# Product 1 of a two-product kernel written out in another order, with its row and column sums taken elsewhere

## The reference, cut to what matters

```python
# x (2, 1024, 2048), ctx (2, 2048, 2048), all float32; s1, z1, s2, z2, g1, g2 are scalars
def fake_quant(x, s, z):
    return (clip(round(x / s + z), 0, 255) - z) * s
x = x + tanh(g1) * matmul(fake_quant(layernorm(x), s1, z1), fake_quant(ctx, s2, z2))   # product 1
h = layernorm(x)
base = h @ base_W.T                                          # (2048, 2048): product 2
logits = h @ router_W.T                                      # 8 experts, the best two are kept
mid = einsum('bsd,edr->bser', h, lora_A) * weights_of_the_best_two
inc = einsum('bser,erd->bsd', mid, lora_B)
out = x + tanh(g2) * (base + 2.0 * inc)
```

## Time and profile before

| | |
|---|---|
| median of 3 runs | 1163.9 us (1162.96 to 1165.37) |
| span of the profiled execution | 1164.5 us (the profile gives no other time of its own for it) |
| PE busy in the span | 1085.9 us, 93% |
| DVE, ACT, POOL busy | 594.8 us, 297.2 us, 189.4 us |
| first unit of product 1 starts | 34.67 us |
| last unit of product 1 ends, product 2's first transposes start | 306.2 us |
| PE busy in the 271.6 us between | 237.9 us |

### The profile page before, as it was taken

The page is one execution under the profiler, slowest core; times in us unless marked ns, Lnnn a source line. Parts: engine busy times, 40 slices in busy tenths (PEclk is TensorE's granted clock), DMA queues, the critical chain, the costliest instruction groups (busy, mean ns, idle before and its releaser), DMA issues.

```text
span 1164.5 us, 13520 instructions
## 1 busy us (share of the span) xinstructions
PE 1085.9 (93%) x5130; PEld 816.5 (70%) x5152; DVE 594.8 (51%) x876; ACT 297.2 (26%) x291; POOL 189.4 (16%) x123
## 2 busy tenths in 40 slices
PE   1678987989999999998999999989999999999998
PEld 1333433334688888887888887878888789888887
DVE  7999698976763543343237224334533343222231
ACT  6642344310241212231112113111211321111210
POOL 3766678662300000000000000000000000000000
PEclk9999998999999999999999999999999999999999
DMA  9885997647572633507242633351542614162440
GB/s 361 299 298 179 311 327 224 236 147 256 190 262 67 200 116 105 194 23 291 73 153 70 211 99 118 132 212 55 181 144 73 199 40 142 54 203 84 148 145 37
DMA packets 111051, 193.88 MB, mean 166 GB/s; under 512 B 30608, under 2 KB 32656, under 8 KB 106896
## 3 DMA queue, kind: packets, MB, share of 16 engines
q1 hardware_dynamic: 68368, 153.18, 38.1%
q10 hardware_dynamic: 42624, 39.85, 11.0%
HBM read 153.16 MB, written 33.55 MB: 160 GB/s over the span
## 4 chain that ended last, share of the span: by engine, by line
PE 71%; DVE 10%; issue 6%; POOL 6%; DMA 4%; ACT 1%; SPq 1%; ACTq 0%; DVEq 0%; POOLq 0%
PE acc L818 17%; PE acc L820 17%; PE acc L819 17%; PE acc L795 3%; POOL ctx_quant L380 3%; PE acc_even L818 3%; PE acc_even L819 3%; PE acc_even L820 3%; DMA w_stage<-in_wt 2%; DVE bn_chunks L540 2%; DVE ctx_tree_sums L591 2%; PE aT_psum L855 1%; PE aT_psum L856 1%; POOL x_group_odd L394 1%; PE aT_psum L833 1%
## 5 line engine op out<-in xcount | busy, mean ns | idle before, releaser
L818 PE MATMUL acc<-w_hi,hT_hi 128*128 128x512 f32 x896 | 353.8, 395 | 0.0
L820 PE MATMUL acc<-w_hi,hT_lo 128*128 128x512 f32 x896 | 350.3, 391 | 0.0
L819 PE MATMUL acc<-w_lo,hT_hi 128*128 128x512 f32 x896 | 349.9, 390 | 0.0
L667 DVE TENSOR_TENSOR w_lo<-w_stage,w_hi 128x1024 fp32r<-128x1024 f32 x128 | 156.6, 1224 | 320.7 <-ACT w_hi L476 318.6
L476 ACT ACTIVATE w_hi<-w_stage 128x1024 fp32r<-128x1024 f32 x128 | 135.6, 1059 | 460.3 <-PE acc L820 314.2
L820 PEld LDWEIGHTS acc<-w_hi,hT_lo 128*128 128x128 f32 x896 | 168.8, 188 | 35.9
L819 PEld LDWEIGHTS acc<-w_lo,hT_hi 128*128 128x128 f32 x896 | 169.0, 189 | 34.2
L818 PEld LDWEIGHTS acc<-w_hi,hT_hi 128*128 128x128 f32 x896 | 168.8, 188 | 33.9
L795 PE MATMUL acc<-ctx_quant,aT_even 128*128 128x512 bf16 x501 | 121.2, 401 | 10.4 <-DVE x_group_even L611 7.9
L795 PE MATMUL acc<-ctx_quant,aT_odd 128*128 128x512 bf16 x501 | 113.7, 383 | 5.0 <-DVE x_group_odd L611 4.4
L795 PEld LDWEIGHTS acc<-ctx_quant,aT_even 128*128 128x128 bf16 x512 | 52.0, 103 | 77.5 <-issue 21.8
(11 more groups left out here) (129 smaller groups left out, 1011.8 us busy)
## 6 DMA issues: line engine op xcount, KB each, us to landing
w_stage<-in_wt SPq DMA_DIRECT2D x128, 512.0 KB, 5.8
ctx_stage<-in_ctx SPq DMA_DIRECT2D x32, 1024.0 KB, 6.5
x_group_even<-x_scratch SPq DMA_DIRECT2D x16, 1024.0 KB, 10.4
residual<-x_scratch SPq DMA_DIRECT2D x64, 256.0 KB, 4.0
out<-residual ACTq DMA_DIRECT2D x64, 256.0 KB, 2.8
x_group_even<-in_x SPq DMA_DIRECT2D x8, 1024.0 KB, 9.0
x_group_odd<-in_x SPq DMA_DIRECT2D x8, 1024.0 KB, 8.1
x_scratch<-x_group_even ACTq DMA_DIRECT2D x8, 1024.0 KB, 4.9
```

What stands on the lines that cost most here:

```text
L667: dve.tensor_tensor(wl[s][:, :], wst[s][:, :], wh[s][:, :].bitcast(F32), ALU.subtract)\
L818: pe.matmul(out_, lh, rh, start=first, stop=False)
L819: pe.matmul(out_, lh, rl, start=False, stop=False)
L820: return pe.matmul(out_, ll, rh, start=False, stop=final)
```

## The change

The change replaces the tables and touches these parts:

- The units come in another order. Before, all four tiles of a group meet block 0, then block 1, and so on. Now the order mixes tiles and blocks within a batch (`UNIT_TILE`, `UNIT_BLOCK`), and the banks go round by position. The loads of SP are in an order of their own (`LOAD_ORDER`).
- Rows: the widening of 8 of the 16 tiles (3, 4, 5, 6, 11, 13, 14, 15) is an ACTIVATE with a row sum on ACT instead of a TENSOR_SCALAR on DVE. The small instruction for the row term stays on DVE and is now apart (`row_sum`). `a_rows` and `x_u8` have two buffers each.
- Three tiles instead of four are transposed on PE; the other 13 by DMA.
- Columns: DVE makes only the first of the four tree instructions (4096 wide, `pair`), and eight matmuls with ones, added up in PSUM, replace the one. The column term is kept for each of the four blocks of a batch, so it is made 8 times instead of 16.

```diff
-PE_TILES = 4
+PE_TILES = 3
+WIDEN_ACT = [3, 4, 5, 6, 11, 13, 14, 15]
+LOAD_ORDER = 'xcxccxccccxccxcccxccccxxccccxcxcxcxcccxccxcxcccx'
+UNIT_TILE = [0, 1, 2, 1, 2, 0, 3, 2, 3, 0, 4, 1, 0, 5, 3, 3, 1, 2, 5, 6, 7, 5, 4, 7, 6, 6, 7, 6, 7, 4, 5, 4, 8,
...
+UNIT_BLOCK = [0, 0, 0, 1, 1, 1, 1, 2, 0, 2, 2, 2, 3, 1, 2, 3, 3, 3, 0, 1, 3, 3, 0, 0, 0, 2, 1, 3, 2, 3, 2, 1, 4,
...
-        anat = at("a_rows", SMALL, [P, D], BF16)
-        xu8 = at("x_u8", SMALL + 4 * KIB, [P, D], U8)
-        csum = at("ctx_part_sums", SMALL + 6 * KIB, [P, NB, NW], F16)
-        tree = at("ctx_tree_sums", SMALL + 10 * KIB, [P, K // 2, NW], F16)
-        colb = [at(f"col_term{s}", SMALL + 18 * KIB + 2 * KIB * s, [P, NW], F32) for s in range(2)]
+        anat = [at(f"a_rows{s}", SMALL + 4 * KIB * s, [P, D], BF16) for s in range(2)]
+        xu8 = [at(f"x_u8_{s}", SMALL + 8 * KIB + 2 * KIB * s, [P, D], U8) for s in range(2)]
+        pair = at("ctx_pair_sums", SMALL + 12 * KIB, [P, K // 2, NW], F16)
+        colb = [at(f"col_term{s}", SMALL + 20 * KIB + 2 * KIB * s, [P, NW], F32) for s in range(NB)]
...
                 if c >= NB:
-                    pool.wait_ge(pe_unit, M * (c + 1))
+                    pool.wait_ge(pe_unit, last_of_block(c - NB) + 1)
+                    pool.wait_ge(block_ready, c - NB + 1)
...
+            def x_widen(t):
+                act.wait_ge(xu8_ready, t + 1)
+                if 2 <= t < PE_TILES + 2:
+                    act.wait_ge(tp_ready, t - 1)
+                elif t >= 2:
+                    wait_aT(act, t - 2)
+                act.activation(anat[t % 2][:, :], xu8[t % 2][:, :], ACT.Identity, bias=-MID,
+                               accum_out=asum[:, t:t + 1]).then_inc(a_by_act, 1)
...
             def store_x1(i):
                 g, n = i // NB, i % NB
-                act.wait_ge(x1_ready, M * (i + 1))
+                act.wait_ge(x1_ready, max(PLACE[M * g + m, NB * (g // 2) + n] for m in range(M)) + 1)
...
+            def row_sum(t):
+                wait_widened(dve, t)
+                dve.tensor_scalar(crow[:, t:t + 1], asum[:, t:t + 1], cd2, ckd, ALU.mult, ALU.add)\
+                    .then_inc(row_ready, 1)
 
             def ctx_sums(c):
-
                 dve.wait_ge(c_conv, CP * (c + 1))
                 if c >= 1:
-                    dve.wait_ge(block_ready, c)
+                    dve.wait_ge(col_ready, c)
+                src = ctxq[:, c % NB, :, :]
+                dve.tensor_tensor(pair[:, :, :], src[:, 0:K // 2, :], src[:, K // 2:K, :], ALU.add)\
+                    .then_inc(block_ready, 1)
...
-                src, w = ctxq[:, c % NB, :, :], K // 2
-                while w:
-                    dst = tree[:, 0:w, :] if w > 1 else csum[:, c % NB, :].unsqueeze(1)
-                    ins = dve.tensor_tensor(dst, src[:, 0:w, :], src[:, w:2 * w, :], ALU.add)
...
+            def col_sums(c):
+                pe.wait_ge(block_ready, c + 1)
+                if c >= 1:
+                    pe.wait_ge(colb_ready, c)
+                for k in range(K // 2):
+                    ins = pe.matmul(colp[:, :], ones[:, :], pair[:, k, :], start=(k == 0), stop=(k == K // 2 - 1))
+                ins.then_inc(col_ready, 1)
...
-B0 = 755
+B0 = 2466
+STEP = 10
...
-                if B0 + 1 <= s <= B0 + M:
-                    group_stats(link, 0, s - B0 - 1)
-                    group_mean_var(link, s - B0 - 1)
+                b = (s - B0) // STEP
+                if 1 <= b <= M:
+                    group_stats(link, 0, b - 1)
+                    group_mean_var(link, b - 1)
```

More of the change, by code:

```diff
@@ L71 @@
-COL_SLOT = [77, 120, 174, 192, 256, 286, 303, 345, 417, 467, 498, 577, 637, 657, 702, 795]
-AFTER = dict(scale=12, quantise=10, widen=24, transpose=16, copy_aT=28, row_term=36,
-             sums=34, col_term=24, add_col=35, evac=26, store=60)
-UNIT_AT, TILE_AT, PIECE_AT, COL_AT = ({slot: i for i, slot in enumerate(table)}
-                                      for table in (UNIT_SLOT, TILE_SLOT, PIECE_SLOT, COL_SLOT))
-SLOTS = max(UNIT_AT) + max(AFTER.values()) + 1
-B0 = 755
+LOAD_ORDER = 'xcxccxccccxccxcccxccccxxccccxcxcxcxcccxccxcxcccx'
@@ L250, in build, with wait_widened, wait_aT @@
         out_stored = [sem(f"out_stored{m}") for m in range(M)]
+        def wait_widened(eng, t):
+            if t in WIDEN_ACT:
+                eng.wait_ge(a_by_act, sum(w <= t for w in WIDEN_ACT))
+            else:
+                eng.wait_ge(a_by_dve, sum(w <= t and w not in WIDEN_ACT for w in range(TILES)))
+        def wait_aT(eng, t):
+            if t < PE_TILES:
+                eng.wait_ge(aT_ready, t + 1)
+            else:
+                eng.wait_ge(aT_moved[t % 2], 16 * sum(w % 2 == t % 2 for w in range(PE_TILES, t + 1)))
         def h_psum(g, k):
@@ L488, in _ @@
                 if k == 1:
-                    store_x1(ITS - 1)
+                    store_x1(LAST_STORE)
                 if k in W_AT:
```

278 lines of the change are left out of this document (146 added, 132 removed), and 9 rows, old and new, of tables (COLADD_SLOT, EVAC_SLOT, UNIT_SLOT).

## The result

The changed kernel is slower: 1181.6 us median of four runs (1179.28 to 1186.19), against 1164.6 (1162.96 to 1167.82) for the kernel before, ratio 1.0142 with a 95% interval of 1.0121 to 1.0164. I had forecast 1151 and given "slower" a chance of 0.13. The profiled execution of the changed kernel took 1179.28 us with a span of 1177.6; it is the fastest of the four. In the larger sets of runs to which the ratios of the experiments refer, the kernel before has a median of 1164.9 to 1165.9 us.

A forecast was written before the change was run, and what follows sets the result against it. DVE's queue was taken to set PE's pace in product 1. Its end: 44 + 222.8 (PE's units and column sums) + 4.2 + 9.2 + 5.1 + 8 = 293.3 us, 12.9 earlier, so 1151 us; range 1140 to 1164.

The forecast's parts named there:

- other waits and slow clock: Product 1, from unit 3 on: 43.2 us before the change, 8 us expected to remain, bounds 0 and 43.
- slow units: Product 1: each of three waits brings a slow unit behind it, 3 x 1.7 = 5.1 us.
- What bounds the kernel: Product 1, up to 306.2 us: DVE's queue (tree, column term, late evacs) sets PE's pace; no engine is full.
- From there on PE is the bound and its work is the same in both: Behind 306.2 us (product 2): time unchanged, so the change gains only what product 1's end moves.
- ACT's widening at 2.1 us: Product 1, ACT: eight widenings moved from DVE at 2.1 us each, 17 us in all, mostly beside other work.
- Column sum at 1.73 us on PE: Product 1, PE: column sums by 64 matmuls instead of 16, 13.8 us instead of 3.5; 1.73 per block.
- Unit 3 at 44: Start of product 1's fourth unit, after the eighth context piece: 44 us, between 40.7 and 48.8.
- Block 5, 4.2 us: Start of second batch: block 5's pieces wait for unit 31, so PE waits 4.2 us, bounds 3 and 8.
- The end, 4.1 and 5.0 us: Product 1's last units: 61 and 62 wait for evacs behind DVE's group 0 chain; 9.2 us lost, bounds 5 and 14.
- ACT's queue: Slower rival: 17 us of widenings delay context pieces and transposes in ACT's queue; decides from 13 us more on PE; chance 0.09.
- The DMA rival: Up to unit 32 in product 1: DMA engines become the bound, time 1158 to 1166; chance 0.15.
- My signs for a wrong forecast: Product 1: PE's waits between above 20 us, put down to `ctx_quant` or a transposed tile, or last units running through.

The follow-up runs named there:

- e9: The combined version e8 with DVE making the whole tree of column sums again and one matmul with ones replacing eight: 1153.6 us.
- e10: The combined version e8 with all 16 widenings back on DVE and none on ACT: 1150.7 us.
- e1: The kernel before with 55 more do-nothing instructions ahead of PE's loop, nothing else changed: 1176.9 us, ratio 1.0096 to the kernel before.
- e6: Changed kernel with PE's loop written out, plus units 27/31 exchanged and unit 36 moved behind the next two: 1157.7 us.
- e7: Changed kernel with PE's loop written out, plus the last even-group unit at 49 instead of 53 and DVE's group 0 chain spread between evacs: 1150.6 us.
- e11: The combined version e8 with tile 5's DMA transpose issued behind context pieces 14 and 15, and unit 13 behind units 14 and 15: 1136.8 us.
- e5: Changed kernel with PE's loop written out, plus group 3's loads held on SP until tile 11 is transposed: 1150.7 us.
- e12: The combined version e8 with loads of tiles 14 and 15 behind the last context pieces and held until tile 12 is transposed: 1145.0 us.
- e15: Changed kernel, PE's loop kept, with group 3's four loads held until tile 11 is transposed: 1176.3 us, ratio 1.01 to the kernel before.
- e2: Changed kernel with 32 more instructions ahead in PE's program, loop kept: 1182.6 us.
- e13: The kernel before with 87 more instructions ahead in PE's program, loop kept: 1168.7 us, ratio 1.0027 to the kernel before.
- e14: Changed kernel with 64 more instructions ahead in PE's program, loop kept: 1169.7 us, ratio 1.0036 to the kernel before.
- e16: Changed kernel, loop kept, with group 3's loads held and 32 more instructions ahead of PE's loop: 1166.6 us, ratio 1.001 to the kernel before.
- e8: Changed kernel with PE's loop written out, combining e5's held loads, e6's unit exchanges and e7's reordered end: 1144.1 us.

## Why the prediction was wrong, step by step

Two steps failed. The sum had 8 us for "other waits and slow clock" in product 1, which with the slow units came out 14.8 us higher. And it took the time behind 306 us for the same in both kernels, which came out 11.1 us longer.

- **What bounds the kernel**: right up to 306 us. PE's waits on DVE's tree and column term went to zero, and each half of the relief is worth something by itself (e9, e10).
- **"From there on PE is the bound and its work is the same in both"**: wrong, 11.1 us. The work is the same and its place in PE's program is not (e1 shows it without the change). The kernel before showed the wait behind each jump back (7.7 us); I had not read the rows behind 306 us, since nothing there was changed.
- **ACT's widening at 2.1 us**: 1.91 and 0.19 for reading the sum, 2.10. The rule of the Trainium skill ("ScalarE: Activation LUTs", section "Rules for kernel authors") would have had this operation stay on DVE; here it takes 2.28 there and 2.10 on ACT, and moving it back cost 6.5 us (e10).
- **Column sum at 1.73 us on PE**: 195.53 to 197.26 in the changed kernel, 1.73.
- **Unit 3 at 44**: 46.25, 2.3 late, inside the bounds.
- **Block 5, 4.2 us**: 3.75, right in size. The cause that I named was only a part: with unit 31 out of the way 3.3 us stayed (e6), and the last piece then waited for ACT.
- **The end, 4.1 and 5.0 us**: 3.04 and 4.43, at the two units that I named, by the chain that I named; taking it away brought 7.7 us (e7).
- **"Other waits and slow clock": 8 us, with 5.1 for slow units, in all 13.1**: this is the failed term. From the measured start of unit 3, 46.25 + 222.8 + 3.75 + 7.47 = 280.3, and product 1 ended at 308.2, so it was 27.9, 14.8 more. Waits are 6.79 (unit 12), 8.32 (unit 36), 3.48 (unit 43) and 0.64, in all 19.2. The rest, 8.7, is mostly slow clock: the units behind four of the waits took 1.7 to 1.9 us longer than the rate gives. I had three such units at 1.7, so that price was right and the waits are what I had too low. I took DVE's share of busy time for the measure of what would be left; but these waits hang on ACT's queue and on transfers.
- **The rival "ACT's queue"**, at 0.09, came nearest, with its place (transposes and pieces in one queue) right and its price wrong: not the 17 us of widenings (e10), but an issue of 5.2 us ahead of two pieces (e11: 7.3 us) and a transpose that lands 13 us after its issue (e5: 7.6 us). "13 us more on PE than I count" was the mark, and it was 14.8.
- **The DMA rival** (all transfers together as a bound) did not come about: unit 32 started at 160.45, and the DMA share up to there was 0.85, where it was 0.84 in the kernel before over the same time. The DMA engines counted in another way: by what was in flight when one short transfer was urgent (e5).

My signs for a wrong forecast were right: PE's waits between were above 20 us (22.3 with block 5), put down to `ctx_quant` or a transposed tile. The 11 us of product 2 had no sign among them.

## What to carry to other kernels

When a change adds or removes instructions of an engine that later runs a loop of over a thousand instructions, read that engine's rows behind each jump back before the forecast: moving the loop by 55 instructions cost 11 us, moving it on by 32 more gave 8 of them back, and writing the loop out took 15 us off the kernel before, as it stood. A short transfer that an engine waits for is priced by what the queues carry at that moment, and its issue holds everything behind it in the issuing engine's queue; put what is urgent ahead of the issue (e11) and hold bulk loads until it has landed (e5), but look at what the held loads will then meet (e12). A share of busy time says how much relief there is, not which waits stay.

## What the runs showed of the hardware

- A jump back of PE's loop costs 3.7 to 4.6 us before its first matmul, in every looped kernel here, and a second wait of 1.6 to 3.1 us came after eight matmuls where the loop started at one place (the changed kernel, e1, e15). In e2, e13, e14 and e16, with the loop 32 or 64 instructions further on, there was none. The granted clock falls with them: it was 0.50, the lower level of 1.2 GHz, from 547.3 to 553.8 us in the changed kernel. The Trainium skill ("Runtime: NRT & Kernel Launch", section "Instruction fetch mechanics") says that instructions come in blocks of 256 and that a taken branch outside the window waits for a fetch. The traces agree: the instruction queue moves packets of 16 KB (0.77 MB in 47 of them in the changed kernel), one of them landed 1.2 to 1.7 us before each of these waits ended, and the second wait stands behind the same eight matmuls in all three kernels whose loop starts at that place.
- A DMA transpose of 128 x 2048 bf16 landed 4.3 us after its issue at best in the changed kernel. That of tile 11 took from 13.2 (e14) to 25.6 us (e6) in six kernels with 1 MB loads going out behind it, and 4.3 in e5, e8 and e15, where they were held. The issue of one took from 1.33 to 10.6 us of ACT's queue.
- An ACTIVATE of 128 x 2048 from uint8 to bf16 with a row sum takes 1.91 us and 0.19 for reading the sum; the same on DVE takes 2.28 us and 0.08.
